# Edge records of a graph network: assembled beside the position step, stored in edge order, and loaded whole for the scatter

## The chip, the cores and the metric

The kernel runs on one core of a Trainium2 chip. The metric is the device time of one execution in microseconds (us). The core has five engines that run programs of their own: TensorE (PE), VectorE (DVE), ScalarE (ACT), GpSimd (POOL) and SyncE (SP). They wait for each other through semaphores. Transfers are run by 16 DMA engines, and are issued from SP's queue or from POOL's.

## The reference

A graph of 6250 nodes (features of 64) and 206250 edges goes through four layers, each followed by a layer norm. Cut to what matters here:

```python
edge_index = jnp.stack([src, dst])                 # edges sorted by dst
x = _layernorm(x + L0(x))                          # two GIN layers: segment_sum(x[src], dst)
x = _layernorm(x + L1(x, edge_attr_64))            # segment_sum(x[src] + x[dst] + edge_attr, dst)
# L2: an MLP on every edge, summed by src (row), edge_weight and edge_attr_16 in it
    row, col = (edge_index[0], edge_index[1])
    d_raw = (edge_weight / CUTOFF)[:, None]
    edge_input = jnp.concatenate([x[row], x[col], edge_attr, d_raw], axis=-1)
    m_ij = silu(silu(edge_input @ ew1 + eb1) @ ew2 + eb2)
    agg = jax.ops.segment_sum(m_ij, row, num_segments=x.shape[0])
# L3: a filter layer, summed by src
```

L2 needs the edges grouped by `src`, while they come sorted by `dst`. So the kernel builds for each edge a record of 32 floats (128 bytes): the 16 edge attributes, the weight over the cutoff, the `dst` number, the low seven bits of `src`, and zeros. It scatters the records to DRAM, in order of blocks of 128 source nodes.

## The kernel before

The stages run one after another. Those up to `plan_windows` are separate blocks in which all engines meet at the end. From `edge_sums` to the last `in_pass` the stages are in one block (`Together`): there PE, ACT, DVE and SP meet after each stage, and POOL does not. POOL runs one long program beside them, `scatter_records`, and all five meet again before the edge MLP.

- `check_order` loads `src`, `dst` and weights as 125 partitions of 1650 edges. The flag `unsorted` is 0 for these inputs, so `sort_in` does nothing.
- `tables_in` (lines 512 to 515) writes on DVE three columns per edge into `edge_meta`, an SBUF tile of 125 x 1650 x 3.
- `count_out` counts the edges of each source block. `place_out` (line 926 on) is the place stage: DVE runs `position_step` (lines 262 to 268) 49 times over 125 x 1650 elements, then six more instructions (956 to 961), which give `edge_row`, the row that each edge's record goes to. Beside it SP writes 104 transfers of padding over the whole target (line 938).
- `plan_windows` prepares index tables.
- `edge_sums` (the sums stage, PE line 1125) sums the 64-wide attributes with 3328 recorded matmuls; DVE makes its one-hot tiles. `build_counts` (the build stage, PE line 1239) fills a count matrix. `in_pass` (line 1324) multiplies that matrix with node features: three times, named sum_x, sum_y and sum_x again, of 2744 matmuls each. sum_x is the first.
- `scatter_records` (line 962 on) works off the 1650 columns in 66 rounds of 25, with three buffers. A round has two parts. `stage` loads the 16 attributes of 25 x 125 edges from the input (line 986, runs of 64 bytes into records of 128), and copies the columns of `edge_meta` (987) and the row numbers (988). `send` issues 25 indirect transfers (line 995), each of which writes 128 records of 128 bytes to 128 rows of `out_records`. The stage of a round is issued ahead of the send of the round before it.

The order on POOL is thus written by hand; it waits in `stage` for the send of three rounds ago, and in `send` for its own load.

## Time and profile before

| what | us |
|---|---|
| median of 3 runs (8381.32 to 8397.97) | 8389.6 |
| profiled execution | 8421.46 |
| its span, first to last instruction | 8419.8 |

The terms below are read in the profiled execution, which is 31.9 us above the median. A change that is worked out there is taken off the median. The busy shares over the span are PE 64%, DVE 40%, ACT 18%, POOL 48%. They are averages over stages with different limits, so the stages are read one by one.

### The profile page before, as it was taken

What the parts mean: (1) busy time and instruction counts of PE and PEld (TensorE: products, weight loads), DVE (VectorE), ACT (ScalarE), POOL (GpSimd) and SP (SyncE); (2) the same over time, 40 slices, a digit from 0 to 9 for tenths busy, and PEclk for the clock granted to TensorE, in tenths of its full rate; (3) what the DMA queues carried; (4) which work ended last, traced back from release to release, by engine and by line L of the source; (5) the groups of instructions that cost most, each with busy time, mean ns of one, the idle gap of its engine ahead of it and who ended that gap; (6) DMA issues with size and microseconds to landing.
All of it is one profiled execution on the core that took longest, in us unless ns stands there. A gap on an engine that the chain in (4) does not pass through costs nothing. (4 is left out here: it accounts for less than half of the span.)

```text
span 8419.8 us, 126717 instructions
## 1 busy us (share of the span) xinstructions
PE 5386.0 (64%) x41112; PEld 4568.4 (54%) x41114; DVE 3363.1 (40%) x5566; ACT 1494.3 (18%) x2045; POOL 4024.6 (48%) x3580
## 2 busy tenths in 40 slices
PE   0004997765552433368776777777777777777696
PEld 0003997522221222258775667777766767666596
DVE  7996332566663000002322333333333333333333
ACT  0000000366656000000001111111111111111242
POOL 0003888888888777720003555444555555552000
PEclk9995555688886655578887888888898888887797
DMA  1203554333334443338763222222222222222584
GB/s 67 74 1 66 90 90 73 67 89 88 89 89 121 111 85 81 80 132 328 273 260 85 77 76 75 75 76 76 76 78 75 76 76 77 75 75 45 105 232 108
DMA packets 907313, 840.43 MB, mean 100 GB/s; under 512 B 326598, under 2 KB 816114, under 8 KB 903661
## 3 DMA queue, kind: packets, MB, share of 16 engines
q1 hardware_dynamic: 788028, 684.65, 26.4%
q0 software_dynamic: 119216, 154.89, 10.5%
q8 instruction: 41, 0.67, 0.0%
q14 instruction: 28, 0.22, 0.0%
HBM read 680.88 MB, written 156.42 MB: 99 GB/s over the span
## 5 line engine op out<-in xcount | busy, mean ns | idle before, releaser
L1736 POOL DMA_INDIRECT edge_mlp_b_rows<-b_table,edge_mlp_recs x1664 | 1631.0, 980 | 2438.5 <-DMA edge_mlp_recs<-out_records 1920.2
L995 POOL DMA_INDIRECT out_records<-nodes_scatter_recs,nodes_scatter_rows x1650 | 2023.3, 1226 | 493.5 <-issue 493.5
L1324 PE MATMUL sum_x_p_main<-sum_x_parts,sum_x_tiles 128*128 128x192 bf16 x5488 | 623.5, 268 | 763.6 <-issue 576.7
L1790 PE MATMUL edge_mlp_p_pre<-edge_mlp_hot_t,edge_mlp_a_blk 128*128 128x128 f32 x3328 | 792.5, 326 | 337.2 <-DVE edge_mlp_hot_t L1850 192.3
L1850 DVE CAST edge_mlp_hot_t<-edge_mlp_p_turned 128x512 f32<-128x512 bf16 x416 | 287.8, 692 | 1762.3 <-PE edge_mlp_p_turned L1782 856.6
L1324 PEld LDWEIGHTS sum_x_p_main<-sum_x_parts,sum_x_tiles 128*128 128x128 f16 x5488 | 506.7, 105 | 880.5 <-issue 872.4
L1239 PE MATMUL build_p_ring<-build_hot_near,build_hot_far 128*128 128x392 f16 x2400 | 616.5, 392 | 432.0 <-issue 235.0
L1759 PE MATMUL edge_mlp_p_m<-edge_mlp_w,edge_mlp_h 128*128 128x128 f32 x3328 | 659.2, 322 | 290.2 <-ACT edge_mlp_h L1817 266.7
L1790 PEld LDWEIGHTS edge_mlp_p_pre<-edge_mlp_hot_t,edge_mlp_a_blk 128*128 128x128 f32 x3328 | 616.2, 231 | 379.8 <-DVE edge_mlp_hot_t L1850 206.2
L1125 PE MATMUL sums_p_sum<-sums_attr,sums_hot 128*128 x3328 | 718.1, 416 | 67.6 <-issue 67.3
L1791 PE MATMUL edge_mlp_p_pre<-c_ident,edge_mlp_b_rows 128*128 128x128 f32 x3328 | 755.0, 314 | 0.0
L1125 PEld LDWEIGHTS sums_p_sum<-sums_attr,sums_hot 128*128 128x128 f32 x3328 | 714.2, 332 | 71.8 <-issue 71.7
L1759 PEld LDWEIGHTS edge_mlp_p_m<-edge_mlp_w,edge_mlp_h 128*128 128x128 f32 x3328 | 554.2, 209 | 352.1 <-ACT edge_mlp_h L1817 302.8
L1239 PEld LDWEIGHTS build_p_ring<-build_hot_near,build_hot_far 128*128 128x128 bf16 x2400 | 255.7, 107 | 792.5 <-issue 740.2
L1791 PEld LDWEIGHTS edge_mlp_p_pre<-c_ident,edge_mlp_b_rows 128*128 128x128 f32 x3328 | 617.3, 231 | 0.0
L1770 PE MATMUL edge_mlp_p_sum<-edge_mlp_m,edge_mlp_hot 128*128 128x128 f32 x3328 | 525.7, 305 | 97.2 <-ACT edge_mlp_m L1811 90.7
L1168 DVE TENSOR_TENSOR nodes_wide_sums<-nodes_wide_sums,edge_mlp_p_sum 128x128 f32 x1664 | 473.5, 285 | 182.6 <-PE edge_mlp_p_sum L1770 3.9
L1221 DVE TENSOR_TENSOR build_hot_near<-c_iota_wide,plan_of_key 128x3136 f16<-128x3136 f16 x300 | 535.7, 1786 | 0.0
L1770 PEld LDWEIGHTS edge_mlp_p_sum<-edge_mlp_m,edge_mlp_hot 128*128 128x128 f32 x3328 | 443.2, 207 | 163.1 <-ACT edge_mlp_m L1811 109.6
L1811 ACT ACTIVATE edge_mlp_m<-edge_mlp_p_m 128x512 f32<-128x512 f32 x416 | 248.5, 597 | 1560.4 <-remote 862.9
L1817 ACT ACTIVATE edge_mlp_h<-edge_mlp_p_pre,edge_mlp_b 128x512 f32<-128x512 f32 x416 | 285.7, 687 | 1131.7 <-remote 564.6
L1091 DVE TENSOR_TENSOR sums_hot<-c_iota,near_of_item 128x1024 f32<-128x1024 f32 x208 | 254.4, 1227 | 509.1 <-PE sums_p_sum L1125 273.6
(443 smaller groups left out, 6597.4 us busy)
## 6 DMA issues: line engine op xcount, KB each, us to landing
sum_x_tiles<-edge_counts SPq DMA_DIRECT2D x168, 768.0 KB, 6.2
edge_mlp_a_blk<-a_table SPq DMA_DIRECT2D x1664, 64.0 KB
edge_counts<-build_plane SPq DMA_DIRECT2D x28, 3136.0 KB
sum_z_tiles<-edge_counts SPq DMA_DIRECT2D x49, 1792.0 KB, 8.8
sum_y_tiles<-edge_counts SPq DMA_DIRECT2D x84, 768.0 KB, 6.3
sums_attr<-in_edge_attr SPq DMA_DIRECT2D x100, 512.0 KB
sum_x_tiles<-edge_counts SPq DMA_DIRECT2D x56, 832.0 KB, 6.3
out_records<-place_padding SPq DMA_DIRECT2D x104, 256.0 KB, 2.1
```

The lines of the kernel that those rows point to most:

```text
L995: pool.indirect_dma_start(out=out_rec, out_offset=bass.IndirectOffsetOnAxis(ap=rows[s][:, c:c + 1], axis=0), in_=recs[s][:, c], in_offset= ...
L1125: mm = pe.matmul(flat[:, ds(sums[c], F + 1)], hot[s][:, c], attr[:, ds(places[c], 1)].rearrange("p o f -> p (o f)"), start=False, stop=Tru ...
L1168: dve.tensor_tensor(dst, dst, psum[:, c:c + 1, 0:width], ALU.add).then_inc(added[s], 1)
L1221: dve.tensor_tensor(hot_near[s][:], bc(k["iota_wide"][:], 1, BATCH // 2), bc(key, 2, KEYS), ALU.is_equal).then_inc(hots_made[s], 1)
L1239: pe.matmul(p_ring[:, ds(banks[c], 1), 0:KEYS], hot_far[s][:, c // 2, :, c % 2], hot_near[s][:, c // 2, :, c % 2], start=False, stop=True, ...
L1324: mm = pe.matmul(p_main[h][:, d, 0:3 * F], tiles[h][u][:, r - cuts[u], d * P:(d + 1) * P], flat[:, r], start=r == 0 and d == 0, stop=r == ...
L1736: pool.indirect_dma_start(out=b_rows[s][:, c], out_offset=None, in_=b_tab, in_offset=bass.IndirectOffsetOnAxis(ap=recs[s][:, c, FE + 1:FE ...
L1759: pe.matmul(p_m[:, c], h[:, c], w2_sb[:], start=True, stop=False)
L1770: mm = pe.matmul(p_sum[s % 2][:, c], hot[s][:, c], m[:, c], start=True, stop=True)
L1790: pe.matmul(p_pre[:, c], a_blk[s][:, c], hot_t[:, c], start=True, stop=False)
L1791: pe.matmul(p_pre[:, c], b_rows[s][:, c], k["ident"][:], start=False, stop=False)
L1850: dve.tensor_copy(hot_t[:], p_hot).then_inc(hot_t_out, 1)
```

## The change

The record columns are no longer kept in `edge_meta`. In the place stage ScalarE builds whole records, 11 pieces of 150 columns for 125 partitions. For a piece SP loads the attributes (125 x 9600 bytes) and stores the finished records (125 x 19200 bytes) to a new DRAM tensor `records`, in edge order, with two buffers of each kind. After that SP writes padding for three spare partitions, and then the 104 transfers of padding as before. In the scatter a round's `stage` loads 25 whole records for all 128 partitions (128 x 3200 bytes, contiguous on both sides), and copies the row numbers. The flag, the second copy of the program behind it and three memsets go from the scatter; two memsets of 125 x 4800 come into the place stage.

```diff
# EdgeArrays: one more tile, low [EP, EC] int32; WIDE = 150
 # tables_in, vector
-            step(dve.tensor_scalar(a.meta[0:EP, :, 0], a.weight[:], 1.0 / CUTOFF, None, ALU.mult))
-            step(dve.tensor_copy(a.meta[0:EP, :, 1].bitcast(I32), a.ends["in"][:]))
-            step(dve.tensor_scalar(a.ints[:], a.ends["out"][:], P - 1, None, ALU.bitwise_and))
-            step(dve.tensor_copy(a.meta[0:EP, :, 2], a.ints[:]))
+            step(dve.tensor_scalar(a.low[:], a.ends["out"][:], P - 1, None, ALU.bitwise_and))
 # place_out
+        attr = [sb(f"attr{s}", [EP, WIDE, FE]) for s in range(2)]
+        recs = [sb(f"recs{s}", [EP, WIDE, OUT_REC]) for s in range(2)]
+        pieces = EC // WIDE
+        lines = lin_rec.rearrange("(p c) w -> p c w", p=P)
         @block.sync
         def _(sp):
+            def assemble(source16):
+                attrs = source16.rearrange("(p c) w -> p c w", p=EP)
+
+                def load(j):
+                    if j >= 2:
+                        sp.wait_ge(made[j % 2], 4 * (j // 2))
+                    sp.dma_start(attr[j % 2][:], attrs[:, j * WIDE:(j + 1) * WIDE]).then_inc(attr_in[j % 2], 16)
+
+                load(0)
+                for j in range(pieces):
+                    if j + 1 < pieces:
+                        load(j + 1)
+                    sp.wait_ge(made[j % 2], 4 * (j // 2 + 1))
+                    sp.dma_start(lines[0:EP, j * WIDE:(j + 1) * WIDE], recs[j % 2][:]).then_inc(stored[j % 2], 16)
...
             sp.wait_ge(pad_set, 2)
+            spare = lin_rec[EP * EC:EP * EC + (P - EP) * EC // P * P].rearrange("(p c) w -> p c w", p=P)
+            for lo in range(0, (P - EP) * EC // P, PRE):
+                width = min(PRE, (P - EP) * EC // P - lo)
+                sp.dma_start(spare[:, lo:lo + width], padding[:, 0:width]).then_inc(prefilled, 16)
+            rest = (P - EP) * EC % P
+            sp.dma_start(lin_rec[P * EC - rest:P * EC], padding[0:rest, 0]).then_inc(prefilled, 16)
             lanes = out_rec[0:P * CHUNKS].rearrange("(p c) w -> p c w", p=P)
             for i in steps(sp, CHUNKS // PRE):
                 sp.dma_start(lanes[:, ds(i * PRE, PRE)], padding[:]).then_inc(prefilled, 16)
...
+        @block.scalar
+        def _(act):
+            act.wait_ge(cleared, 2)
+            for j in range(pieces):
+                s, at = j % 2, slice(j * WIDE, (j + 1) * WIDE)
+                if j >= 2:
+                    act.wait_ge(stored[s], 16 * (j // 2))
+                act.mul(recs[s][:, :, FE], a.weight[:, at], 1.0 / CUTOFF).then_inc(made[s], 1)
+                act.copy(recs[s][:, :, FE + 1].bitcast(I32), a.ends["in"][:, at]).then_inc(made[s], 1)
+                act.copy(recs[s][:, :, FE + 2], a.low[:, at]).then_inc(made[s], 1)
+                act.wait_ge(attr_in[s], 16 * (j // 2 + 1))
+                act.copy(recs[s][:, :, 0:FE], attr[s][:]).then_inc(made[s], 1)
         @block.gpsimd
         def _(pool):
+            for s in range(2):
+                nc.gpsimd.memset(recs[s][:], 0.0).then_inc(cleared, 1)
 # scatter_records, gpsimd: the two programs behind a flag become one
-        for s in range(3):
-            nc.gpsimd.memset(recs[s][:], 0.0).then_inc(cleared, 1)
-        pool.wait_ge(cleared, 3)
             def stage(i, s, done):
                 at = ds(i * (3 * SC) + s * SC, SC)
                 wait_count(pool, scattered[s], done * (16 * SC))
                 turnstile(pool, k["gate"], s, passed)
-                pool.dma_start(recs[s][0:EP, :, 0:FE], recs_of[:, at]).then_inc(rec_in[s], 16)
-                nc.gpsimd.tensor_copy(recs[s][0:EP, :, FE:FE + 3], meta[0:EP, at]).then_inc(staged[s], 1)
+                pool.dma_start(recs[s][:], lines[:, at]).then_inc(rec_in[s], 16)
                 nc.gpsimd.tensor_copy(rows[s][:], row[:, at]).then_inc(staged[s], 1)
```

GpSimd in the scatter, at the head of a round, before:

```order
L986 DMA nodes_scatter_recs<-in_edge_attr 125x25x16
L987 COPY nodes_scatter_recs<-edge_meta 125x25x3
L988 COPY nodes_scatter_rows<-edge_row 128x25
L995 DMA out_records<-nodes_scatter_recs,nodes_scatter_rows 217942x32 x25
L986 DMA nodes_scatter_recs<-in_edge_attr 125x25x16
```

and after:

```order
L1027 DMA nodes_scatter_recs<-records 128x800
L1028 COPY nodes_scatter_rows<-edge_row 128x25
L1035 DMA out_records<-nodes_scatter_recs,nodes_scatter_rows 217942x32 x25
L1027 DMA nodes_scatter_recs<-records 128x800
L1028 COPY nodes_scatter_rows<-edge_row 128x25
```

One copy is gone from each round, and the load has another shape; the 25 scatters stand where they stood.

SP's queue in the place stage, before:

```order
L933 UNCONDITIONAL_BRANCH
L938 DMA out_records<-place_padding 128x512
L194 UNCONDITIONAL_BRANCH
L194 ISA
L938 DMA out_records<-place_padding 128x512
```

and the end of the same program after (the 11 pieces stand ahead of the first row in the same manner):

```order
L951 DMA records<-place_recs 125x4800
L944 DMA place_attr<-in_edge_attr 125x2400
L951 DMA records<-place_recs 125x4800 x2
L957 UNCONDITIONAL_BRANCH
L963 DMA records<-place_padding 128x512 x2
L963 DMA records<-place_padding 128x192
L965 DMA records<-place_padding 86x32
L968 DMA out_records<-place_padding 128x512
```

The padding of `out_records` moved behind 11 loads, 11 stores and 4 transfers of spare padding.

## Rows read from the trace of the kernel before

**Rows 1.** Page, part five: line, engine, operation, tiles | busy us, mean ns

```profile
L995 POOL DMA_INDIRECT out_records<-nodes_scatter_recs,nodes_scatter_rows x1650 | 2023.3, 1226 | 493.5 <-issue 493.5
```

**Rows 2.** Busy time of each engine (instructions) in the place, sums and build stages

```profile
core 0: us, PE busy (x) PEld busy (x) DVE busy (x) ACT busy (x) POOL busy (x), PEclk, DMA share, GB/s
173.70:626.20 452.50, 0.00 (x0) 0.00 (x0) 423.34 (x202) 0.00 (x0) 2.78 (x3) 1.00 0.16 60
784.00:1560.00 776.00, 713.68 (x3309) 709.96 (x3309) 257.47 (x210) 0.00 (x0) 625.83 (x480) 0.50 0.51 83
1560.00:2611.00 1051.00, 619.20 (x2413) 259.20 (x2412) 721.91 (x608) 629.45 (x785) 898.51 (x574) 0.83 0.34 87
```

**Rows 3.** The same of line 1324 alone: sum_y, and sum_x up to the last scatter

```profile
3832.00:4063.00 231.00, 228.26 (x2744) 227.67 (x2744) 0.99 0.92 362
2744.00:3637.00 893.00, 316.24 (x1835) 201.63 (x1836) 0.58 0.40 84
```

**Rows 4.** Timeline: TensorE after the last scatter, VectorE at the end of sum_x

```profile
3644.11 6.10 PE L1324 MATMUL sum_x_p_main<-sum_x_parts,sum_x_tiles 128*128 128x192 bf16 x51 [0.23 <-issue]
...
3720.74 0.56 DVE L1350 TENSOR_REDUCE nodes_in_sums<-sum_x_p_main 128x384 f32 x1 [7.53 <-PE sum_x_p_main L1324]
```

**Rows 5.** Windows inside one scatter round of sum_x, and at the last round

```profile
3323.00:3331.00 8.00, 7.45 (x62) 6.64 (x62) 0.56 (x1) 0.00 (x0) 6.01 (x8) 0.76 0.96 166
3331.00:3355.00 24.00, 5.97 (x25) 2.31 (x25) 0.00 (x0) 0.00 (x0) 18.52 (x20) 0.56 0.36 105
3604.00:3637.00 33.00, 3.83 (x12) 1.36 (x13) 0.00 (x0) 0.00 (x0) 24.96 (x26) 0.50 0.06 13
3637.00:3643.00 6.00, 0.93 (x3) 0.31 (x3) 0.00 (x0) 0.00 (x0) 0.00 (x0) 0.50 0.01 3
```

**Rows 6.** Lines 995 and 986 (ns min/median/max), then the busy sum of line 987

```profile
L995 POOL DMA_INDIRECT out_records<-nodes_scatter_recs,nodes_scatter_rows x1650: 953/962/4074, 818.4 to 3635.7; - x184
...
L986 POOL DMA_DIRECT2D nodes_scatter_recs<-in_edge_attr x66: 3784/3844/3851, 796.7 to 3569.3; - x66
...
sum 2853.00, POOL 37.96; mean POOL 12.65
```

**Rows 7.** Timeline, GpSimd: a scatter issue that meets a VectorE instruction

```profile
1269.00 1.84 POOL L995 DMA_INDIRECT out_records<-nodes_scatter_recs,nodes_scatter_rows  x1 [0.30 <-issue]
```

**Rows 8.** Timeline: copies of stage tables on VectorE, start of the scatter on GpSimd

```profile
36.06 1.27 DVE L512 TENSOR_SCALAR edge_meta<-edges_weight 125x1650 f32<-125x1650 f32 x1 [11.95 <-SPq L506]
...
39.73 1.29 DVE L515 CAST edge_meta<-edges_ints 125x1650 f32<-125x1650 int32 x1
...
784.65 2.17 POOL L976 MEMSET nodes_scatter_recs<- 128x800 f32 x3 [22.94 <-POOLq L183]
796.72 3.84 POOL L986 DMA_DIRECT2D nodes_scatter_recs<-in_edge_attr  x1 [9.89 <-issue]
```

**Rows 9.** Waits of the SP queue; its issue; windows of two kinds of transfer

```profile
SPq L274 <- DMA edges_weight<-in_edge_weight: 18.2, 1, 18.2
...
11.56 1.91 SPq L288 DMA_DIRECT2D edges_weight<-in_edge_weight  x1
...
12.00:31.00 19.00, 0.59 (x2) 0.50 (x2) 5.94 (x8) 0.00 (x0) 0.00 (x0) 1.00 0.31 128
176.00:258.00 82.00, 0.00 (x0) 0.00 (x0) 76.74 (x37) 0.00 (x0) 0.53 (x1) 1.00 0.90 333
```

**Rows 10.** Timeline: end of the place stage; line 1256: ScalarE copies of 784 elements

```profile
624.33 1.88 DVE L961 SCALAR_TENSOR_TENSOR edge_row<-edges_run,edges_eq 125x1650 int32<-125x1650 f32 x1
...
L1256 ACT CAST build_plane<-build_p_ring x448: 812/812/820, 1577.1 to 2707.8; 128x784 f16<-128x784 f32 x150
```

**Rows 11.** Windows of line 1125 alone (sums): before 1305 us, and two slow spells

```profile
800.00:1305.00 505.00, 498.91 (x2333) 497.81 (x2333) 0.50 0.53 90
...
1336.00:1351.00 15.00, 2.68 (x10) 2.88 (x10) 0.50 0.05 12
...
1459.00:1474.00 15.00, 2.56 (x10) 2.46 (x10) 0.50 0.21 46
```

More of the change, by code:

```diff
@@ L934, in _ @@
         def _(sp):
-            sp.wait_ge(pad_set, 2)
+            def assemble(source16):
[10 more added lines that the diff above has]
+                    sp.dma_start(lines[0:EP, j * WIDE:(j + 1) * WIDE], recs[j % 2][:]).then_inc(stored[j % 2], 16)
+            flag = nc.values_load(k["unsorted"][0:1, 0:1], engines=[SP], min_val=0, max_val=E,
+                                  skip_runtime_bounds_check_because="a count of edges")
+            with sp.If(flag > 0):
+                assemble(in_rec[:, F + 2:F + 2 + FE])
+            with sp.Else():
+                assemble(ea16)
+            sp.wait_ge(pad_set, 2)
+            spare = lin_rec[EP * EC:EP * EC + (P - EP) * EC // P * P].rearrange("(p c) w -> p c w", p=P)
[4 more added lines that the diff above has]
+            sp.dma_start(lin_rec[P * EC - rest:P * EC], padding[0:rest, 0]).then_inc(prefilled, 16)
             lanes = out_rec[0:P * CHUNKS].rearrange("(p c) w -> p c w", p=P)
@@ L962, in _, with scatter_records @@
                                           op0=ALU.mult, op1=ALU.add))
[L965 to L971 removed]
+def scatter_records(nc, k, together, recs, rows, row, lin_rec, out_rec, signals):
+    rec_in, staged, passed, scattered = signals
+    lines = lin_rec.rearrange("(p c) w -> p c w", p=P)
     @together.block.gpsimd
     def _(pool):
[L975 to L1008 removed]
@@ new lines, in stage, with send @@
+        def stage(i, s, done):
+            at = ds(i * (3 * SC) + s * SC, SC)
+            wait_count(pool, scattered[s], done * (16 * SC))
+            turnstile(pool, k["gate"], s, passed)
+            pool.dma_start(recs[s][:], lines[:, at]).then_inc(rec_in[s], 16)
+            nc.gpsimd.tensor_copy(rows[s][:], row[:, at]).then_inc(staged[s], 1)
+        def send(i, s):
+            pool.wait_ge(rec_in[s], i * 16 + 16)
+            pool.wait_ge(staged[s], i + 1)
+            turnstile(pool, k["gate"], s, passed)
+            for c in range(SC):
+                pool.indirect_dma_start(
+                    out=out_rec, out_offset=bass.IndirectOffsetOnAxis(ap=rows[s][:, c:c + 1], axis=0),
+                    in_=recs[s][:, c], in_offset=None).then_inc(scattered[s], 16)
@@ L1009, in scatter @@
+        rounds = PIECES // 3
+        stage(0, 0, 0)
+        for i in steps(pool, rounds - 1):
             stage(i, 1, i)
@@ L1012, in scatter @@
             send(i, 1)
+            stage(i + 1, 0, i + 1)
             send(i, 2)
-        flag = nc.values_load(k["unsorted"][0:1, 0:1], engines=[POOL], min_val=0, max_val=E,
-                              skip_runtime_bounds_check_because="a count of edges")
-        with pool.If(flag > 0):
-            scatter(in_rec[:, F + 2:F + 2 + FE])
-        with pool.Else():
-            scatter(ea16)
+        i = rounds - 1
+        stage(i, 1, i)
+        send(i, 0)
+        stage(i, 2, i)
+        send(i, 1)
+        send(i, 2)
         for s in range(3):
@@ L2033, in right @@
                 return to.enter_context(nc.sbuf_tensor(name, shape, dt, side="right"))
-            meta, row = right(both_ctx, "edge_meta", [P, EC, 3]), right(both_ctx, "edge_row", [P, EC], I32)
-            signals = [ctx.enter_context(nc.semaphore(n)) for n in ("recs_cleared", "recs_passed")]
+            row = right(both_ctx, "edge_row", [P, EC], I32)
+            passed = ctx.enter_context(nc.semaphore("recs_passed"))
             rec_in, staged, scattered = ([ctx.enter_context(nc.semaphore(f"recs_{n}{s}")) for s in range(3)]
```

47 lines of the change are left out of this document (12 added, 35 removed).

## The prediction

> **What bounds the kernel now.** The page's groups come first. Line 995, the scatter's indirect transfers, keeps GpSimd busy for 2023.3 us [rows 1], and what ends its idle time is "issue": it waits for no transfer. Next come windows by stage. In the place stage VectorE is busy 423.34 of 452.50 us, ScalarE not at all, the DMA engines 0.16 [rows 2]: room beside a chain on VectorE. In the sums and build stages TensorE works through its matmuls while the scatter runs beside it.
>
> The question is where the scatter's length reaches the end of the kernel. It issues from 796.7 to 3635.7 [rows 6], into sum_x. The windows of line 1324 show it: sum_y does its 2744 matmuls in 231 us, 0.0842 us each; sum_x, the same program beside the scatter, does 1835 in 893 us [rows 3]. The timeline shows TensorE with a run of 51 matmuls at 3644.11, some 8 us after the last indirect issue, and the last reduce of sum_x at 3720.74 [rows 4]. The 909 matmuls left, at 0.0842 us, take 76.5 us, and 3637 + 6 + 76.5 is 3719.5. So the end of sum_x is the scatter's end, plus 6, plus what is left at full pace. All later stages wait for sum_x and none for the scatter itself.
>
> Inside a round of sum_x TensorE isn't held evenly. In 8 us right behind the round's load it does 62 matmuls, in the next 24 us 25, and in the last round, where no load follows, 12 in 33 us [rows 5]. The fast spell comes while GpSimd's queue has had a pause of some 4 us, the issue of the load.
>
> **The change part by part.** All sums are made in the profiled execution (8421.46 us, span 8419.8). It lies 31.9 us above the median of the runs; I take the difference off the median.
>
> *tables_in.* Three of four VectorE instructions go: the first at 36.06 took 1.27 us, the last at 39.73 took 1.29 [rows 8]. That is 3.8 us and the gaps between them, 4 us off everything.
>
> *Start of the scatter.* Three memsets, 2.17 us together, go. Behind them stand 9.89 us without an instruction, in which GpSimd reads the flag and branches [rows 8]. Some of that is the loop's own start; bounds 0 and 9.9, I take 5. Together 7 us.
>
> *The round's load.* It is issued 66 times at 3.84 us [rows 6], a group that scarcely varies. The old load has 3125 pieces of 64 bytes, the new one 128 of 3200. No such load stands in the trace. Above, its issue costs what the old one does, 3.84; below, nothing. The nearest row is an indirect issue, also with 128 pieces on each side, median 0.96 [rows 6]. I take 1.0, since both load the queue with as many pieces: 66 x 2.84 is 188 us less (bounds 0 and 253). The Trainium skill, "DMA: Bandwidth & Descriptors", section "Anatomy of one DMA", speaks against this term: by it the number of descriptors hardly moves the fixed cost until it is large. By it the issue would stay near 3.84 and this term near nothing; the two rows, 3.84 and 0.96 for unequal numbers of pieces, speak against it here.
>
> *The copies of line 987.* 37.96 us of GpSimd's time [rows 6] go.
>
> *What comes back.* An issue that meets a VectorE instruction takes 1.84 us instead of 0.96 [rows 7]; the mean of 1226 ns over all 1650 against a median of 962 [rows 1, 6] says how common that is. So far some of VectorE's instructions fell into the 3.84 us of the load or the copy, where they cost nothing seen. Now they meet an indirect issue: about one more per round in the 42 rounds beside sums and build, 42 us, and some 18 us for what the shorter copies leave. Bounds 0 and 66 x 1.84 = 121; I take 60, one collision of 0.9 us in each round.
>
> Sum for the end of the scatter: -4 -7 -188 -38 +60 = -177, from 3637 to 3460. The copy of row numbers stays, and the order of stage and send too, so no new wait stands in the loop.
>
> *What TensorE makes of it.* If it depends on the pause at the load, the shorter load takes much of the fast spell away. Without spells the pace was (1835 - 25 x 62) / (25 x 28) = 0.41 per us; right behind them 1.04 [rows 3, 5]. I take 0.7, since a pause of 1 to 1.5 us with the copy remains. From 2740 to 3460 that makes 504 matmuls, and 2240 are left: 189 us. The end of sum_x is 3460 + 6 + 189 = 3655, against 3720.7: **-65 us**. With 0.41 it is 3672 (-49), with 1.04 3634 (-87). The slower pace thus gives back 113 of 177 us: a matmul not done beside the scatter costs 0.084 us after it.
>
> *Records in the place stage.* GpSimd first clears two tiles of 125x4800; three memsets of 128x800 took 2.17 us [rows 8], so 2 x 4.3, about 9 us ahead of ScalarE's start and of the padding. Per piece ScalarE writes 2400 elements and three times 150. Its copies of 784 elements took 812 ns [rows 10]; by size 2.5 us and some 0.7, so 3.2 us per piece, beside the transfers. SP moves 11 x (1.2 + 2.4) = 39.6 MB from and to 125 partitions. The row for that shape is the three loads of 125 x 6600 bytes: 128 GB/s with a DMA share of 0.31, from 12 to 31 us; SP waited 18.2 us for them [rows 9]. That gives 309 us (11 pairs of 9.4 and 18.7). Load j+1 is issued before SP waits for ScalarE's piece j, so ScalarE's 3.2 us lie under a transfer; were they bare, 35 us more. Then come the spare padding, 4 us, and the old padding, 82 us at 333 GB/s [rows 9]. So 174 + 9 + 309 + 4 + 82 = 578, or 613 with ScalarE bare, against VectorE's end at 626.2 [rows 2, 10]. It is hidden, with 13 to 48 us to spare; beyond that each us counts in full. The Trainium skill, "DMA: Bandwidth & Descriptors", section "Why a DMA increments its semaphore by 16 and not by 1", says that the partition count must divide by the number of engines used, so 125 gives 5 of 16. The share of 0.31 is 5 of 16; by the page's 27 GiB/s per engine the 309 us would be an estimate of 273, and nothing in the sum would change.
>
> VectorE itself isn't slowed by transfers: under the padding at a share of 0.90 it was busy 76.74 of 82 us [rows 9], 0.936, as over the whole stage [rows 2]. The memsets touch at most 9 us of it; bounds 0 and 9, I take 0 to 1.
>
> **Rivals.**
>
> *TensorE keeps its spells (a).* If they come from the round itself, not from the length of the pause, 2.06 matmuls per us [rows 3] go on: 1483 done by 3460, 1261 left, 106 us, end 3572, -149: 8241 us. For it: a load and a copy still stand between two sends. Against it: in the last round, without a load, there is no spell [rows 5], and the spell is the length of what the pause could refill.
>
> *The load's issue keeps its price (b).* Then the scatter gains 4 + 7 + 38 and loses some 20 in collisions: 29 earlier. At the pace of before, 60 fewer matmuls are done: -29 + 5 = -24, 8366 us. The change then does only half of what it says.
>
> *Slower: the sums stage falls into its slow spell (c).* Up to 1305 TensorE did 2333 matmuls in 505 us, 4.6 per us; but from 1336 to 1351 it did 10 in 15 us, and again from 1459 to 1474 [rows 11]. Both spells ended as the next round's load was issued. With a short pause they may not end. Beginning at 1305 with 976 to do, 0.67 per us takes 1457 us: the stage ends at 2762 instead of 1560. The scatter is over long before sum_x then; sum_x starts at 3946, takes 231 us and ends at 4177: +456, 8846 us. It decides only from a point: the scatter's end hides any delay until sum_x starts later than 3489, 745 us late. Smaller losses in sums and build cost almost nothing. For it: the same symptom in another stage. Against it: two spells only in the 776 us of the stage.
>
> *Slower: the place stage overruns (d).* If ScalarE, SP and the transfers go at half the rate of the row, 618 us instead of 309, the stage ends at 887 instead of 626: +261, 8586 with the forecast's gain. It starts to cost at 1.16 times my time for the pieces and eats the gain at 1.37 times. Against it: the same shape stood in the trace at full rate, in loads; for it: stores to DRAM from 125 partitions did not.
>
> **How the numbers follow.** What a measurement of this kernel can tell from no change is some 0.2%, 17 us. The forecast, 8389.6 - 65 = 8325 (8300 to 8345 by the pace and the collisions), has a chance of 0.52; (a) 0.17; (b) 0.15, of which half is near no change; (c) 0.11, (d) 0.05. Faster by over 0.2%: 0.52 + 0.17 + 0.07 = 0.76; within 0.2%: 0.08; slower: 0.16. The range takes in (a), with a load issue of half my price (33 us, of which 27 arrive), and (b) up to no gain at all, and leaves out (c) and (d): 8215 to 8400.
>
> **What would show it.** Right: the last indirect issue near 3460; the load's issue near 1 us; line 995's mean a little above 1226 ns; sum_x with about 500 matmuls done at the scatter's end and then 190 us at full pace; ScalarE idle again and the padding landed before 600. Wrong: an issue of 3.8 us (b); over 1200 matmuls done beside the scatter (a); a sums stage longer than 776 us by hundreds (c); position_step's last instruction before SP's last landing (d). If the scatter's end moved as forecast but the end of sum_x did not, the law "end plus what is left" is wrong.

## The result and the profile after

| | us |
|---|---|
| kernel before, median of 8 | 8389.98 (8381.32 to 8401.92) |
| changed kernel, median of 8 | 8418.83 (8365.60 to 8427.08) |
| ratio | 1.0029, 95% interval 1.0016 to 1.0042 |
| changed kernel, profiled execution | 8365.6, span 8363.9 |

In this comparison the changed kernel is 0.3% slower, where 8325 us and a gain of 65 had been forecast. The profiled execution of the changed kernel is the shortest of its eight, 53 us under the median, while that of the kernel before lay above its own. So totals are compared by the medians, and the profiles are read stage by stage. Up to the end of sum_x the two profiles differ by 4.2 us; the edge MLP, whose code isn't touched, is 43 us shorter in the profile after (from its first to its last matmul 3194 us, before 3236).

The page of the changed kernel, fifth part, the line that answers to [rows 1]. GpSimd's issues became longer on the mean, 1266 ns for 1226. Its idle time ahead of them, for which the profile names no cause ("issue"), grew from 493.5 to 537.3 us:

```profile
L1035 POOL DMA_INDIRECT out_records<-nodes_scatter_recs,nodes_scatter_rows x1650 | 2088.5, 1266 | 537.3 <-issue 537.3
```

The scatter's two lines one by one (ns min/median/max, first and last start), which answer to [rows 6]:

```profile
L1035 POOL DMA_INDIRECT out_records<-nodes_scatter_recs,nodes_scatter_rows x1650: 952/958/4086, 792.7 to 3493.9; - x184
```

```profile
L1027 POOL DMA_DIRECT2D nodes_scatter_recs<-records x66: 572/580/595, 786.7 to 3425.1; - x66
```

The load's issue fell from 3.84 to 0.58 us, and the last indirect issue from 3635.7 to 3493.9. That is 142 us, of which 4 arrived at the end of sum_x. Windows of TensorE's line 1357 (sum_x and sum_y; the columns are PE, weight loads, clock, DMA share, GB/s), as in [rows 3]:

```profile
3020.00:3494.00 474.00, 61.55 (x217) 23.63 (x217) 0.50 0.13 36
3494.00:3500.00 6.00, 0.64 (x2) 0.26 (x3) 0.50 0.02 5
3500.00:3717.00 217.00, 212.33 (x2525) 211.53 (x2525) 0.98 0.92 359
3828.00:4061.00 233.00, 229.39 (x2744) 228.71 (x2742) 0.99 0.91 359
```

Beside the scatter TensorE did 217 matmuls of sum_x, where it had done 1835 before [rows 3]; 2525 were left. The timeline shows the last reduce of sum_x, 4.2 us before that of [rows 4]:

```profile
3716.50 0.56 DVE L1383 TENSOR_REDUCE nodes_in_sums<-sum_x_p_main 128x384 f32 x1 [7.53 <-PE sum_x_p_main L1357]
```

And it shows how TensorE gets on while GpSimd issues. Each row is one instruction (start, us):

```profile
3152.12 0.96 POOL L1035 DMA_INDIRECT out_records<-nodes_scatter_recs,nodes_scatter_rows  x1 [0.30 <-issue]
3152.59 0.32 PE L1357 MATMUL sum_x_p_main<-sum_x_parts,sum_x_tiles 128*128 128x192 bf16 x1 [2.48 <-issue]
3153.51 0.95 POOL L1035 DMA_INDIRECT out_records<-nodes_scatter_recs,nodes_scatter_rows  x1 [0.43 <-issue]
3153.99 0.10 PEld L1357 LDWEIGHTS sum_x_p_main<-sum_x_parts,sum_x_tiles 128*128 128x128 f16 x1 [2.70 <-issue]
3154.92 0.95 POOL L1035 DMA_INDIRECT out_records<-nodes_scatter_recs,nodes_scatter_rows  x1 [0.46 <-issue]
3155.39 0.32 PE L1357 MATMUL sum_x_p_main<-sum_x_parts,sum_x_tiles 128*128 128x192 bf16 x1 [2.48 <-issue]
```

TensorE starts one instruction every 1.4 us, a weight load and then a matmul. That is one matmul in 2.8 us, 0.36 per us. Both engines wait for "issue", neither for a semaphore or a transfer. I call TensorE held in this state. The granted clock doesn't explain it: it is 0.50 here, and in the sums stage, at 0.50 too, TensorE did 3328 matmuls in 711 us.

In these rows an instruction of TensorE stands 0.47 us behind the start of each issue, as if each issue let one through; so do the expectations below put it. The end of the scatter in the kernel before shows that it is not so:

```profile
3634.46 0.96 POOL L995 DMA_INDIRECT out_records<-nodes_scatter_recs,nodes_scatter_rows  x1 [0.30 <-issue]
3635.01 0.32 PE L1324 MATMUL sum_x_p_main<-sum_x_parts,sum_x_tiles 128*128 128x192 bf16 x1 [2.48 <-issue]
3635.72 0.96 POOL L995 DMA_INDIRECT out_records<-nodes_scatter_recs,nodes_scatter_rows  x1 [0.30 <-issue]
3636.41 0.10 PEld L1324 LDWEIGHTS sum_x_p_main<-sum_x_parts,sum_x_tiles 128*128 128x128 f16 x1 [2.69 <-issue]
3637.81 0.32 PE L1324 MATMUL sum_x_p_main<-sum_x_parts,sum_x_tiles 128*128 128x192 bf16 x1 [2.48 <-issue]
3639.21 0.10 PEld L1324 LDWEIGHTS sum_x_p_main<-sum_x_parts,sum_x_tiles 128*128 128x128 f16 x1 [2.69 <-issue]
3640.61 0.32 PE L1324 MATMUL sum_x_p_main<-sum_x_parts,sum_x_tiles 128*128 128x192 bf16 x1 [2.48 <-issue]
3642.01 0.10 PEld L1324 LDWEIGHTS sum_x_p_main<-sum_x_parts,sum_x_tiles 128*128 128x128 f16 x1 [2.70 <-issue]
```

GpSimd issues every 1.26 us, TensorE starts one instruction every 1.40 us, and it keeps that step for 6 us when no issue comes any more. In the changed kernel, from 3040 to 3494 us, 286 of TensorE's 338 steps are 1.4 us, 35 are 0.7 and 13 are 2.1. So the issues don't set the step; they keep the state going, and it ends some microseconds after they stop. GpSimd can fall into the same step, and then the gap ahead of its issue is 0.43 to 0.46 us instead of 0.30: this is so for 117 of its 320 steps from 3040 to 3494, and for 1 of 616 in sum_x of the kernel before, though TensorE is held for most of each round there too.

A slow spell of the same look stands in the build stage, from 1515 to 1930 us (columns PE, weight loads, VectorE, ScalarE, GpSimd, clock, DMA share, GB/s), against [rows 2]:

```profile
794.00:1505.00 711.00, 710.23 (x3328) 710.05 (x3328) 250.72 (x205) 0.00 (x0) 585.24 (x452) 0.50 0.42 93
1515.00:1930.00 415.00, 81.06 (x176) 18.61 (x176) 59.01 (x53) 44.14 (x55) 317.74 (x320) 0.50 0.13 34
1970.00:2858.00 888.00, 522.55 (x2186) 223.88 (x2184) 649.68 (x544) 575.02 (x717) 755.77 (x478) 0.90 0.26 96
```

The sums stage lost its slow spells and ended 60 us earlier; the build stage met one of 415 us, with 176 matmuls, and sum_x began at 3020 instead of 2744. As long as that is under 3489 it costs little: the scatter sets the end.

The place stage did what was forecast: ScalarE's large copy takes 2192 ns, the last store of records is issued at 434.4, the last padding at 544.6, and VectorE ends at 626 as before. The windows of the stage (same columns) show the transfers at 5 of 16 engines, and the time behind them empty:

```profile
184.00:436.00 252.00, 0.00 (x0) 0.00 (x0) 235.70 (x111) 31.96 (x41) 0.00 (x0) 1.00 0.32 135
560.00:627.00 67.00, 0.00 (x0) 0.00 (x0) 61.89 (x33) 0.00 (x0) 0.00 (x0) 1.00 0.00 0
```

### The profile page after: what moved, and what is told of

It is laid out like the page before. It is cut to its first block and busy times, and to the rows that moved or that the text cites. A ratio compares the mean times of both kernels' runs of the same rounds, so it can differ in the third digit from the quotient of the medians.

```text
span 8363.9 us, 126665 instructions
## 1 busy us (share of the span) xinstructions
PE 5253.3 (63%) x41112; PEld 4503.5 (54%) x41114; DVE 3362.9 (40%) x5563; ACT 1528.2 (18%) x2089; POOL 3862.2 (46%) x3513
## 5 line engine op out<-in xcount | busy, mean ns | idle before, releaser
L1035 POOL DMA_INDIRECT out_records<-nodes_scatter_recs,nodes_scatter_rows x1650 | 2088.5, 1266 | 537.3 <-issue 537.3
L1357 PE MATMUL sum_x_p_main<-sum_x_parts,sum_x_tiles 128*128 128x192 bf16 x5488 | 503.3, 251 | 635.3 <-issue 581.0
L1357 PEld LDWEIGHTS sum_x_p_main<-sum_x_parts,sum_x_tiles 128*128 128x128 f16 x5488 | 463.7, 99 | 675.0 <-issue 673.8
L1803 PE MATMUL edge_mlp_p_sum<-edge_mlp_m,edge_mlp_hot 128*128 128x128 f32 x3328 | 507.9, 298 | 80.8 <-ACT edge_mlp_m L1844 73.3
L1803 PEld LDWEIGHTS edge_mlp_p_sum<-edge_mlp_m,edge_mlp_hot 128*128 128x128 f32 x3328 | 426.2, 200 | 142.9 <-ACT edge_mlp_m L1844 90.6
L1289 ACT CAST build_plane<-build_p_ring 128x784 f16<-128x784 f32 x448 | 364.6, 814 | 704.3 <-PE build_p_ring L1272 533.4
```

The costliest lines, as they stand in the source:

```text
L1035: pool.indirect_dma_start(out=out_rec, out_offset=bass.IndirectOffsetOnAxis(ap=rows[s][:, c:c + 1], axis=0), in_=recs[s][:, c], in_offset= ...
L1289: act.copy(to, ring.rearrange("p b (r d) -> p b r d", d=WIN)).then_inc(copied, 1)
L1357: mm = pe.matmul(p_main[h][:, d, 0:3 * F], tiles[h][u][:, r - cuts[u], d * P:(d + 1) * P], flat[:, r], start=r == 0 and d == 0, stop=r == ...
L1803: mm = pe.matmul(p_sum[s % 2][:, c], hot[s][:, c], m[:, c], start=True, stop=True)
```

## The experiments

Two theories stood against each other. **The hold:** TensorE beside the scatter is held to single instructions; a pause between the issues lets it run for some microseconds; the change shortened the pause, and so gave away in matmuls what it won in the scatter. **Something else:** the small-piece traffic, the copies, a spell in the build stage that lasts too long, or a later stage.

Kernels that were measured together, the kernel before always among them, form a session (the expectations say "call"). The sessions differ, and this was a finding. Each run is compared with the kernel before in its own session:

| session | kernel before, us | run | us | ratio (95%) |
|---|---|---|---|---|
| 1 | 6579.9 | before_cut | 4459.6 | 0.6773 (0.6757 to 0.6790) |
| | | after_cut | 4279.8 | 0.6499 (0.6486 to 0.6512) |
| | | after_pieces | 6462.0 | 0.9809 (0.9791 to 0.9828) |
| | | after_again | 6406.6 | 0.9728 (0.9711 to 0.9746) |
| 2 | 8234.6 | before_again | 8233.6 | 0.9997 (0.9981 to 1.0012) |
| | | after_pause | 8212.9 | 0.9960 (0.9940 to 0.9980) |
| | | after_64 | 8735.1 | not comparable, see there |
| | | before_nometa | 8613.6 | not comparable, see there |
| 3 | 8407.9 | before_3 | 8403.3 | 0.9995 (0.9982 to 1.0007) |
| | | after_3 | 8414.8 | 1.0005 (0.9994 to 1.0017) |
| | | pauses4 | 7888.1 | 0.9382 (0.9366 to 0.9399) |
| | | pauses4s | 7861.0 | 0.9342 (0.9324 to 0.9361) |
| 4 | 6576.8 | before_4 | 6578.1 | 1.0000 (0.9989 to 1.0011) |
| | | after_4 | 6402.8 | 0.9731 (0.9717 to 0.9744) |
| | | before_pauses | 6718.9 | 1.0208 (1.0194 to 1.0222) |
| | | pauses6 | 6537.5 | 0.9934 (0.9920 to 0.9947) |
| 5 | 8224.8 | before_pauses_2 | 7838.5 | 0.9520 (0.9488 to 0.9553) |
| 6 | 8386.9 | pauses4s_2 | 7827.1 | 0.9345 (0.9324 to 0.9365) |

**Sessions 1 and 4: no hold.** 

> The kernel before with the edge MLP left out (its block sums are set to zero instead): the time of everything else. From the trace of before, 8389.6 less the 3236 us of the edge MLP and its start, about 5150. It is here to be compared with after_cut in the same call.

```diff
-        edge_mlp(nc, k, out_rec, a_tab, b_tab, wide, ew1, eb1, ew2, eb2)
+        with nc.Block() as cut:
...
+                dve.memset(wide_sums[:], 0.0)
```

> The changed kernel with the same part left out. Theory one (the stages up to sum_x end alike, at 3720.7 before and 3716.4 after, because a shorter pause takes from TensorE what the earlier end of the scatter gives): within 6 us of before_cut, 4 us shorter if anything, and the 29 us that the whole kernel is longer lie in the edge MLP. Theory two (in most executions TensorE's slow spell in the build stage lasts beyond the point from which it decides, sum_x starting at 3489): over 20 us longer than before_cut, with a wide spread.

> The changed kernel unaltered, for a second profile: whether the stages up to sum_x end at 3716 again, and whether the slow spell of the build stage (1504 to 1930) has the same place and length. Theory one: sum_x ends within 15 us of 3716 whatever the spell does, and the edge MLP (3194 us from its first to its last matmul in the first profile, 3236 before) carries what is left, 3194 to 3250.

The expectations were written for 8390 us, and the session gave 6580. In it TensorE is never held. after_cut is 180 us shorter than before_cut, and the whole changed kernel 173: the edge MLP takes 2120 and 2127 us by the difference, so all of the gain lies ahead of it. Neither theory had foreseen this; both had taken the state of the first traces for granted. Session 4 repeated the pair, with a whole profile of each.

> The kernel before unaltered, partner of the other runs of this call. Where TensorE is held beside the scatter, the end of sum_x by the number of matmuls a pause lets through: 3640 to 3730.

> The changed kernel unaltered. Where TensorE is held: 0.37 matmuls per us in sum_x and its end at 3700 to 3735; the whole kernel behind before_4 by the difference of the two ends, give or take 15 us: about equal where before_4 lets 66 to 74 matmuls a pause through, 50 to 70 us slower where it lets 100. The rival, that the first comparison's 29 us lay in a later stage: the difference of the wholes isn't that of the ends of sum_x. Where it isn't held: 170 to 180 us faster.

The scatter's line in before_4, and then in after_4:

```profile
L995 POOL DMA_INDIRECT out_records<-nodes_scatter_recs,nodes_scatter_rows x1650: 952/959/4085, 807.2 to 3644.7; - x184
```

```profile
L1035 POOL DMA_INDIRECT out_records<-nodes_scatter_recs,nodes_scatter_rows x1650: 954/959/4087, 780.7 to 3464.8; - x184
```

The scatter ends 180 us earlier (forecast 177, and 3464.8 against a forecast of 3460; that it fits so well is luck in part, see below). The windows of sum_x, of the in_pass line alone, first in before_4, where the scatter's loads come in pieces of 64 bytes, and then in after_4:

```profile
2676.00:2942.00 266.00, 238.03 (x2744) 233.58 (x2744) 0.96 1.01 342
```

```profile
2598.00:2830.00 232.00, 228.56 (x2744) 227.92 (x2744) 0.99 0.97 388
```

Without the hold sum_x takes 266 and 232 us beside the scatter, not 977 and 697. The third pass ended at 3638.2 with the scatter's last issue at 3644.7 in before_4, and at 3464.6 and 3464.8 in after_4. Behind it the next stage starts in both. So the two chains end together, moved by 174 and 180 us, and the kernel by 175 (0.9731). Where nothing holds TensorE the change is worth 2.7%. The two sessions also show where the hold costs: against before_4 the first profile of the kernel before is 711 us longer in sum_x and 1128 in the edge MLP, which is nearly all of the difference of 1843.

> The changed kernel with one size altered: the buffers of the scatter have rows of 33 floats, so that the round's load has 3200 pieces of 128 bytes on its inner side instead of 128 of 3200; all else stays. Theory one: the issue goes back from 0.58 to about 3.9 us, TensorE does some 60 matmuls behind each load in sum_x again (2.07 per us instead of 0.37), the slow spell of the build stage is gone or under one round, the scatter ends 100 to 200 us later than 3494 and the end of sum_x stays within 30 us of 3716. A rival, that the relief in sum_x came from the transfer's small 64-byte writes or from the copies of line 987 and not from the pause: the issue returns, and TensorE stays at 0.37 per us, with the end of sum_x near 3800.

```diff
-            recs = [sb(f"scatter_recs{s}", [P, SC, OUT_REC]) for s in range(3)]
+            recs = [sb(f"scatter_recs{s}", [P, SC, OUT_REC + 1]) for s in range(3)]
-            pool.dma_start(recs[s][:], lines[:, at]).then_inc(rec_in[s], 16)
+            pool.dma_start(recs[s][:, :, 0:OUT_REC], lines[:, at]).then_inc(rec_in[s], 16)
...
-                    in_=recs[s][:, c], in_offset=None).then_inc(scattered[s], 16)
+                    in_=recs[s][:, c, 0:OUT_REC], in_offset=None).then_inc(scattered[s], 16)
```

Without the hold it could not tell what it was made for. It gave two prices: an issue of 1590 ns (expected 3.9 us), and a scatter that ends at 3526.3 instead of 3464.8, 61.5 us for 66 x 1.0 us, with 55 us of it in the total.

**Session 2: the pause.** 

> The kernel before unaltered, for a second whole profile. The four runs so far were on a chip where the kernel before took 6580 us and the changed one 6407, and where TensorE was never held to one instruction per issue of GpSimd. Expected: either the first state of things (8390 us, sum_x 977 us long, 0.41 matmuls per us outside the spells) or the second (6580 us, sum_x 265 us long); in the second the last indirect issue at 3650 and the stage behind it waiting for that.

> The changed kernel with one addition: behind each round's load GpSimd clears a tile that nobody reads (4200 elements of 16 bits, 2 to 4 us), a pause between the issues with nothing transferred. Where TensorE is held beside the scatter, theory one (the pause lets it go) expects a fast spell of some 60 matmuls behind each pause in sum_x and an end of sum_x within 30 us of 3716; the rival (it is the traffic of the small pieces) expects 0.37 per us still and sum_x's end 150 to 250 us later. Where it isn't held, the scatter is the bound, and 66 pauses cost their sum, 130 to 260 us.

```diff
             pool.dma_start(recs[s][:], lines[:, at]).then_inc(rec_in[s], 16)
+            nc.gpsimd.memset(idle[s][:], 0.0).then_inc(staged[s], 1)
             nc.gpsimd.tensor_copy(rows[s][:], row[:, at]).then_inc(staged[s], 1)
...
-            pool.wait_ge(staged[s], i + 1)
+            pool.wait_ge(staged[s], i * 2 + 2)
```

The hold was there. The timeline of after_pause, round the pause of one round of sum_x:

```profile
3035.06 0.58 POOL L1028 DMA_DIRECT2D nodes_scatter_recs<-records  x1
3035.47 0.32 PE L1359 MATMUL sum_x_p_main<-sum_x_parts,sum_x_tiles 128*128 128x192 bf16 x1 [1.78 <-issue]
3035.63 3.61 POOL L1029 MEMSET nodes_idle<- 128x4200 f16 x1
3036.17 0.10 PEld L1359 LDWEIGHTS sum_x_p_main<-sum_x_parts,sum_x_tiles 128*128 128x128 f16 x1 [1.99 <-issue]
3037.57 0.32 PE L1359 MATMUL sum_x_p_main<-sum_x_parts,sum_x_tiles 128*128 128x192 bf16 x1 [1.78 <-issue]
3038.27 0.10 PEld L1359 LDWEIGHTS sum_x_p_main<-sum_x_parts,sum_x_tiles 128*128 128x128 f16 x1 [1.99 <-issue]
3038.97 5.25 PE L1359 MATMUL sum_x_p_main<-sum_x_parts,sum_x_tiles 128*128 128x192 bf16 x35 [1.08 <-issue]
```

For some 3 us of the pause single instructions still come; then a run of matmuls that outlasts it. The run starts 4.9 us behind the start of the last indirect issue, at 3034.1. The pause transfers nothing, so the small pieces are not needed for the relief. The window of sum_x (line 1359) in after_pause:

```profile
2717.00:3577.00 860.00, 344.70 (x2363) 241.67 (x2361) 0.62 0.34 110
```

2.75 matmuls per us, against 0.38 to 0.46 in the changed kernel without it. The total is 0.9960 of the kernel before, with 1 outside the interval: a pause put back into the changed kernel, for nothing but its length, doesn't cost 66 x 3.9 us but leaves it slightly the faster of the two. Session 2 has no run of the changed kernel without the pause; in session 3 it stood at 1.0005.

before_again was also a warning. Its sum_x did 2501 matmuls in 885 us, 2.8 per us where the first profile had 2.06, and ended at 3654, not 3720:

```profile
2748.00:3633.00 885.00, 355.05 (x2501) 256.63 (x2498) 0.62 0.47 110
```

How much one round of the kernel before lets through differs from session to session: 74 matmuls in the first profile, 76 in before_3, 101 here (pace times 35.8 us).

> The changed kernel with one part undone, the shape of the load: it takes the 16 attributes only, as pieces of 64 bytes (left out: the other columns of the record stay zero, so the edge MLP sums other edges). Issue expected back at 3.84 us, as in the kernel before (3.84 with 3125 pieces of 64 bytes; 1.59 with 3200 of 128; 0.58 with 128 of 3200). Where TensorE isn't held: the scatter ends some 66 x 3.26 = 215 us less what falls on VectorE's instructions, so 150 to 215 us, later than 3465, and the in_pass stages take 264 us instead of 231, as before. Where it is held: fast spells back, end of sum_x within 30 us of 3716.

```diff
+        for s in range(3):
+            nc.gpsimd.memset(recs[s][:], 0.0).then_inc(passed, 1)
...
-            pool.dma_start(recs[s][:], lines[:, at]).then_inc(rec_in[s], 16)
+            pool.dma_start(recs[s][:, :, 0:FE], lines[:, at, 0:FE]).then_inc(rec_in[s], 16)
```

It missed in both respects, and was worth the most. The issue takes 1578 ns, not 3.84 us, for 3200 pieces of 64 bytes, and the hold stays through sum_x as long as the scatter runs (window of its line 1362):

```profile
2682.00:3518.00 836.00, 99.85 (x314) 32.45 (x313) 0.50 0.12 30
```

314 matmuls in 836 us, 0.38 per us. So small pieces without a long issue give no relief, and a long pause without small pieces does: that settles it for the pause. Its total says nothing, since the edge MLP takes every record as one of node 0.

> The kernel before with the copy of line 987 taken out of the rounds (left out: the weight, the number and the low bits of a record stay zero). The 38 us of that copy alone, less collisions that move to other instructions: the scatter ends 15 to 38 us earlier. Where TensorE isn't held the whole time falls by that; where it is, by that less 8%.

```diff
-                nc.gpsimd.tensor_copy(recs[s][0:EP, :, FE:FE + 3], meta[0:EP, at]).then_inc(staged[s], 1)
-                pool.wait_ge(staged[s], i * 2 + 2)
+                pool.wait_ge(staged[s], i + 1)
```

The last indirect issue is at 3605.6 instead of 3633.2 in before_again: 28 us for a copy that was busy 38, as expected. And the copy isn't what relieves TensorE: without it sum_x still does 1993 matmuls from 2750 to 3606, 2.3 per us. The build stage takes 1040 us as before. The total isn't comparable, for the same reason.

**Session 3: more pauses.** 

> The kernel before unaltered, as the partner of after_3 in the same call, each with a whole profile. Where TensorE is held beside the scatter: sum_x ends within 25 us of the scatter's last issue plus 6 plus what is left at 0.0842 us each, between 3640 and 3730 by how many matmuls each pause lets through (62 of 74 a round in the first profile, about 100 in the second).

> The changed kernel unaltered. Where TensorE is held: 0.37 matmuls per us in sum_x, the scatter's end at 3465 to 3500, sum_x's end at 3700 to 3730 whatever the spell in the build stage does; against the kernel before 20 to 60 us slower where that one's pauses let 100 matmuls through, and equal to it where they let 74. The rival (the 29 us of the first result lie behind sum_x, in the edge MLP): the ends of sum_x differ by less than 10 us. Where it isn't held: 170 to 180 us faster.

The windows of sum_x in before_3, up to the scatter's last issue and after it, and then those of after_3:

```profile
2851.00:3629.00 778.00, 276.34 (x1647) 176.47 (x1646) 0.59 0.41 88
3635.00:3723.00 88.00, 86.42 (x1004) 85.09 (x1003) 0.95 0.82 319
```

```profile
2711.00:3519.00 808.00, 97.56 (x308) 31.74 (x308) 0.50 0.13 36
3525.00:3731.00 206.00, 200.29 (x2386) 198.89 (x2385) 0.98 0.90 355
```

The scatter ends 110 us earlier (3519 for 3629), and TensorE has 1382 matmuls more to do behind it: 1382 x 0.0842 is 116 us. sum_x ends at 3723 and 3731, and the changed kernel is at 1.0005 of the kernel before. Here the slow spell of the build stage was missing, and it changed nothing.

> The changed kernel, with four pauses in each of the last 27 rounds (ahead of scatters 0, 6, 12 and 19 GpSimd clears an unread tile of 4200 floats, some 3.6 us). Where TensorE is held: if a pause of 3.6 us lets some 90 to 100 matmuls through wherever it stands, sum_x takes 300 to 450 us instead of 700 to 980, sum_y and the third pass run beside the scatter too, the scatter ends near 3900, and the stages up to the third pass end at 3900 to 4050 instead of 4350: 300 to 450 us faster than both kernels. The rival (the relief belongs to the round's start, a load and a copy ahead of it): 74 to 100 matmuls per round as with one pause, and the end of sum_x later by the pauses, 250 us or more. Where it isn't held: the scatter ends later by 27 x 4 x 3.7 = 400 us, and so does the kernel.

> The same with pauses of half the length (2100 floats, about 1.8 us). In the changed kernel a gap of 0.58 us and a copy let nothing through, and a gap of 4.4 or 3.9 us lets a spell of some 8 us through. If the spell only needs any gap over 1.8 us, the pace is as in pauses4 and the scatter ends 200 us earlier than there, near 3700; if it needs more than that, sum_x runs at 0.37 per us and its end is 3494 + 200 + 6 + 200, near 3900.

```diff
...
+        def pause(before):
+            wait_count(pool, idled, before)
+            pool.sem_inc(passed, 1)
+            nc.gpsimd.memset(idle[:], 0.0).then_inc(idled, 1)
...
             for c in range(SC):
+                if paused and c in (0, 6, 12, 19):
+                    pause(((i - 13) * 3 + s) * 4 + (0, 6, 12, 19).index(c))
```

(`paused` holds from round 39 on; idle is 4200 floats, in pauses4s 2100.) Both are 6% faster than either kernel. GpSimd in pauses4s, timeline, then the windows of sum_x and sum_y in the same kernel:

```profile
2705.88 0.96 POOL L1045 DMA_INDIRECT out_records<-nodes_scatter_recs,nodes_scatter_rows  x1 [0.30 <-issue]
2706.82 1.87 POOL L1036 MEMSET nodes_idle<- 128x2100 f32 x1
2708.87 0.97 POOL L1045 DMA_INDIRECT out_records<-nodes_scatter_recs,nodes_scatter_rows  x1 [0.17 <-POOL nodes_idle L1036]
```

```profile
2660.00:3006.00 346.00, 272.43 (x2729) 247.69 (x2726) 0.90 0.74 262
3125.00:3478.00 353.00, 276.46 (x2744) 250.30 (x2744) 0.90 0.73 258
```

sum_x takes 346 us beside the scatter, at 7.9 matmuls per us, and sum_y runs beside it as well. The scatter ends at 3661 (pauses4: 3840), later than in the changed kernel, and the edge MLP begins at 3942 instead of 4495. The rival, that the relief belongs to the round's start, had expected 250 us more. The forecast of 300 to 450 us was too low: it is 527 to 554.

Note that 1.87 us suffice here, every six scatters, but a gap of 2.0 us once a round (after_64) did not. In pauses4s a pause mostly finds TensorE already running: sum_x begins with 93 matmuls in 11 us (2657 to 2668). But sum_x begins with a run in after_3 too (49 matmuls in its first 25 us), where nothing keeps it up.

**Sessions 4 to 6: what the change is worth beside pauses.** 

> The kernel before with pauses of 2100 floats (1.87 us) ahead of scatters 6, 12 and 19 of the last 27 rounds; ahead of scatter 0 stands its load anyway. It tells what the change itself is worth once TensorE isn't held. Where it was held: if the hold was all that ate the earlier end of the scatter, this kernel is 100 to 170 us slower than the changed kernel with four such pauses (7861 us against 8408 of the kernel before), so 0.95 of the kernel before or 7960 to 8030; if the change is worth nothing even then, it is equal to it, 0.935. The scatter ends near 3790 against 3661.

> The same kernel as before_pauses, for a chip on which TensorE is held beside the scatter. As there: if the hold was all that ate the earlier end of the scatter, 0.95 of the kernel before (the changed kernel with four pauses was at 0.934); if the change is worth nothing even without the hold, 0.935.

> The changed kernel with four pauses of 1.87 us once more, since its 0.934 and the 0.952 of the kernel before with pauses come from two chips. Where TensorE is held: 0.93 to 0.94 of the kernel before, the edge MLP starting near 3940. Where it isn't: the pauses only cost, as in before_pauses; 27 x 4 x 2.3 us less some 60 for the last of them, so about 190 us above the changed kernel.

> The changed kernel with six pauses of 1050 floats (0.9 us) in each of the last 27 rounds, every four scatters. Pauses of 1.87 us every six scatters kept TensorE at 7 to 8.7 matmuls per us. If its pace goes by the sum of the pauses in a round (5.6 against 7.5 us), it stays above 5 per us and the kernel within 1% of 7861 (0.935). If a pause has to be longer than some 1 us to count, TensorE stays at 0.37 and the kernel is slower than the changed one by the pauses, 27 x 6 x 1.2 = 190 us.

(The same edits as above: in before_pauses and before_pauses_2 in the kernel before, with pauses at 6, 12 and 19; in pauses4s_2 as in pauses4s; in pauses6 in the changed kernel, with six pauses of 1050 floats.) Where TensorE isn't held the pauses only cost: the kernel before goes to 1.0208, the changed one with six pauses from 0.9731 to 0.9934. What pauses of 0.9 us do where it is held stays open, since pauses6 ran in a free session alone. Where it is held, the kernel before with pauses is at 0.952, the changed kernel with pauses at 0.934 and 0.9345. By these ratios the change is worth some 1.8% once the pauses lift the hold, but no session held both kernels, and the kernel before itself differs by 2% between them (8225, 8387 and 8408 us). By the profiles it is 0.9%: the edge MLP starts at 4010 in before_pauses_2 and at 3942 and 3938 in the other two, 70 us; I had expected 100 to 170. The scatter ends 132 us earlier in pauses4s, but in all three TensorE's chain was the later one.

## Why the prediction failed, point by point

**The law of the end held.** Scatter's end, plus 6, plus what is left at 0.0842 us: 3494 + 6 + 213 = 3713 against 3717 here, 3720 against 3723 in before_3, 3726 against 3731 in after_3. The 6 us are the time for which TensorE stays held behind the last issue.

**The first failed step: the scatter's end, 3494 instead of 3460.** The load's issue fell further than assumed: 66 x 3.26 = 215 us, not 188. What comes back was well sized, (1266 - 1226) ns x 1650 = 66 us against 60. By these two the end would be near 3439. The missing 55 us are terms that the sum had at nothing. 44 of them are GpSimd's idle time ahead of the issues, 537.3 us instead of 493.5: where TensorE stays held from round to round, GpSimd is slowed too. after_3 has 549.1 and after_64 534.6, while after_pause (held, with pauses) and after_4 (free) have 494. Rounds of sum_x took up to 38 us where the shortest took 32.2. The other 12 are the copy of the row numbers, which the forecast left as it was: busy 35.0 us instead of 22.6. It grew in the free session as well (36.2 for 16.7), so there the 180 us against a forecast of 177 are errors of opposite sign. Of the page "DMA: Bandwidth & Descriptors" of the Trainium skill the prediction had said that by its section "Anatomy of one DMA" the issue's price would stay. It did not: 3.84 became 0.58 us.

**The second failed step: the pace of TensorE in sum_x, 0.7 matmuls per us.** It was 0.46 here (217 in 474 us) and 0.43 in after_3 (357 in 833), the first burst included, and 0.38 in after_3 without it (308 in 808). The prediction had seen that the pause of the load makes the fast spell and that it would go. But it took half-way between two windows instead of the lower bound, though the last round's 12 in 33 us [rows 5], 0.36, is that of the state without a pause. And it gave the starting point 2740 to sum_x, where a spell in the build stage made it 3020. Together: the scatter is 34 us late, 285 more matmuls are left, 24 us, and 3655 becomes 3713; 3717 was measured. What both steps have in common is that the forecast took the pause as time saved on GpSimd alone, though it had seen that TensorE runs in it.

**Why nothing arrived.** Session 3 has the sum. Behind the start of sum_x a round of before_3 takes 35.8 us and lets 76 matmuls through, a round of after_3 takes 35.4 us and lets some 13 through. So in sum_x the shorter load gains 0.4 us a round and costs 62 matmuls, 5.2 us of TensorE. The scatter was ahead by 101 us when sum_x was young (the loads at 2846.6 and 2745.8), won 8 more in the 20 rounds behind that, and ended 110 ahead; the 1382 matmuls cost 116. What the rounds ahead of sum_x gain, sum_x gives back. No run shows anything that ties the two to each other; that they come out nearly equal looks like chance.

**The 29 us of the first comparison.** They lie in no profile of it. The repeat gives 1.0005, and its interval (0.9994 to 1.0017) just touches 1.0016 to 1.0042, so a part of the 0.3% may be no more than the spread between sessions. That rounds worth 100 matmuls, as in session 2, would put the kernel before 60 to 75 us ahead of 3716 to 3731 fits; which pauses the unprofiled executions had wasn't measured. The cause of that 0.3% stays open between this and the edge MLP, whose length differed by 43 us between two profiles of the same code.

**The rivals.** (a) and (b) were wrong. (c) named the right symptom in the wrong stage: the spell came in the build stage, lasted 415 us, and cost little because sum_x still began before 3489, the point worked out for it. (d) did not happen: the transfers of the pieces ran from 171 to some 464 us, about 293 us (309 forecast), and the padding had landed by 550.

## What to carry to other kernels

When an engine runs slower beside another's issues, look at single instructions in the timeline before costing a change of that other engine. If it steps along one instruction at a time, with no wait that the profile names, find out what ends that state, and whether the change takes it away: here a load that was 3.3 us shorter took away what let TensorE run. Where one of two such engines has long work of its own, a few deliberate pauses in the other's stream can be worth more than any saving: here 27 x 4 pauses of 1.87 us cost the scatter 142 us (3519 to 3661) and gave the kernel 554. Where TensorE isn't held they only cost. And take a range from the state of the machine too: the same kernel took 6577, 8225 or 8408 us in different sessions, and the same change was worth 2.7% or nothing.

## What the runs showed that was not expected

- TensorE beside a stream of indirect issues either runs freely or is held to one instruction per 1.4 us (sometimes 0.7 or 2.1), and whole sessions go one way or the other. Two sessions were on the chip with the same number, 10, one free (6577 us) and one held (8225 us), so it isn't a property of the chip alone. The edge MLP, where GpSimd issues gathers, is 2109 to 2111 us long in free sessions and 3116 to 3236 in held ones. What brings the state about, and what the two engines share, is not in the traces.
- The hold outlasts the last indirect issue. In sum_x of held sessions TensorE's run starts 4.7 to 5.3 us behind the start of that issue in nearly every round (before, before_again, before_3, after_pause), where the next issue comes after 5.4 us or more. Steps of up to 4.2 us between two issues in after and after_64, and one of 4.9 in after_3, brought no run. Staying out of the hold takes less: 1.87 us of pause every six issues.
- The issue of a load by GpSimd took 3.84 us for 125 x 25 pieces of 64 bytes, 1.58 for 128 x 25 of 64, 1.59 for 128 x 25 of 128, and 0.58 for 128 of 3200. So 25 times as many pieces from 128 partitions cost 1.0 us, and 64 or 128 bytes made no difference. The first load has another number of partitions and reads another tensor; which of the two makes the other 2.3 us wasn't taken apart.
- The build stage takes 1035 to 1041 us in every profile whose load has 125 partitions (before_4 and before_nometa among them), and 971 to 983 with any of the loads of 128 (after_4, after_pieces and after_64 among them), with 64-byte pieces as well, but for the first profile with its spell. The trace doesn't name the reason.
